# Routed expert rows weighted on ScalarE and summed into the tokens' rows in memory by an accumulating indirect DMA, in place of a gather and weighted sum in the next stage

## The reference, cut to what matters

```python
def _L0_ffn_ref(x, router_w, router_b, routed_w1, routed_w3, routed_w2, shared_w1, shared_w3, shared_w2):
    def _expert(xf, w1, w3, w2):
        return jax.nn.silu(xf @ w1) * (xf @ w3) @ w2
    xf = x.reshape(T, D)
    logits = xf @ router_w + router_b
    topk_vals, topk_idx = jax.lax.top_k(logits, 2)
    sparse = jnp.full_like(logits, -jnp.inf)
    sparse = sparse.at[jnp.arange(T)[:, None], topk_idx].set(topk_vals)
    gates = jax.nn.softmax(sparse, axis=-1)
    routed = jax.vmap(_expert, in_axes=(None, 0, 0, 0))(xf, routed_w1, routed_w3, routed_w2)   # 8 experts
    routed_out = jnp.einsum('etd,te->td', routed, gates)
    shared_out = jax.vmap(_expert, in_axes=(None, 0, 0, 0))(xf, shared_w1, shared_w3, shared_w2).sum(axis=0)   # 2
    return (routed_out + shared_out).reshape(B, S, D)

x = x + tanh(g_xattn[0]) * _L0_xattn_ref(_layernorm(x), ctx, ctx, ...)
x = x + tanh(g_ffn[0]) * _L0_ffn_ref(_layernorm(x), ...)
x = x + tanh(g_xattn[1]) * _L1_xattn_ref(_layernorm(x), ctx)      # softmax(x ctx^T) ctx
x = x + tanh(g_ffn[1]) * _L1_ffn_ref(_layernorm(x), ...)          # quantised up, conv over the sequence, silu, quantised down
```

## Time and profile before

| what | value |
|---|---|
| three runs | 1677.87, 1670.09, 1670.02 us; median 1670.09 |
| profiled execution | 1673.33 us (its span on the core 1671.7) |
| busy over the span | PE 1510.4 us (90%), weight loads 1147.7, DVE 1053.8 (63%), ACT 815.9 (49%), POOL 743.7 (44%) |
| loop over routed tiles | 69 tiles; first output copy at 744.11, last at about 1079 us |

### The profile page before, as it was taken

One profiled execution on the slowest core, in us unless ns is written; L12 is line 12 of the kernel. 1 busy time (PEld: TensorE's weight loads), 2 busy tenths in 40 slices (PEclk: granted clock), 3 DMA queues, 4 the chain that ended last, 5 costly groups with the idle time before them and its releaser, 6 DMA issues. The chain is left out here.

```text
span 1671.7 us, 24835 instructions
## 1 busy us (share of the span) xinstructions
PE 1510.4 (90%) x8764; PEld 1147.7 (69%) x8764; DVE 1053.8 (63%) x1759; ACT 815.9 (49%) x1448; POOL 743.7 (44%) x666
## 2 busy tenths in 40 slices
PE   6589999999978999989999999988888789999997
PEld 5478788788756888867787788765554455555553
DVE  3468878788728564332332333247996899999995
ACT  2145555555522221213343444325777778888883
POOL 0044344435414675243414100255551878888870
PEclk9789999999978999999999999995766889999998
DMA  3157656666326999735535333459772111111112
GB/s 142 46 182 252 210 207 252 228 212 230 127 85 216 355 356 345 247 120 176 179 105 169 119 107 107 138 145 319 235 258 92 38 39 38 64 63 63 52 51 101
DMA packets 131428, 270.31 MB, mean 162 GB/s; under 512 B 16083, under 2 KB 31443, under 8 KB 129288
## 3 DMA queue, kind: packets, MB, share of 16 engines
q1 hardware_dynamic: 100168, 175.47, 31.2%
q0 software_dynamic: 16624, 62.93, 10.7%
q10 hardware_dynamic: 14544, 30.68, 4.9%
HBM read 145.56 MB, written 122.42 MB: 160 GB/s over the span
## 5 line engine op out<-in xcount | busy, mean ns | idle before, releaser
L243 PE MATMUL e_u_ps<-e_xs,w_shared 128*128 128x512 f32 x720 | 169.4, 396 | 6.4 <-DVE e_sg L1262 6.4
L243 PEld LDWEIGHTS e_u_ps<-e_xs,w_shared 128*128 128x128 f32 x720 | 137.6, 192 | 35.4 <-DVE e_sg L1262 6.5
L2357 PE MATMUL f_banks<-b_xdT,w1h 128*128 128x512 f32 x512 | 146.0, 427 | 14.5 <-POOL b_xdT L2107 9.7
L2133 POOL TENSOR_TENSOR b_h<-b_h,b_srow 128x512 f32<-128x512 f32 x112 | 143.3, 1333 | 26.3 <-ACT b_srow L2169 26.3
L1458 PE MATMUL e_u_ps<-e_w,e_xs 128*128 128x512 f32 x528 | 133.0, 401 | 2.0 <-DVE e_xs L1354 1.2
L2357 PEld LDWEIGHTS f_banks<-b_xdT,w1h 128*128 128x128 f32 x512 | 97.1, 196 | 48.2 <-POOL b_xdT L2107 14.1
L2326 PE MATMUL b_o_ps<-w2q,b_h 128*128 128x512 bf16 x448 | 116.9, 384 | 8.7 <-ACT b_h L2163 8.7
L2158 ACT ACTIVATE b_h<-b_h 128x512 f32<-128x512 f32 x128 | 88.2, 690 | 53.4 <-DVE b_h L2248 52.4
L1362 DVE TENSOR_TENSOR e_hT<-e_r_ps,e_hT 128x256 fp32r<-128x256 f32 x69 | 29.3, 424 | 134.5 <-ACT e_hT L1200 134.5
L1458 PEld LDWEIGHTS e_u_ps<-e_w,e_xs 128*128 128x128 f32 x528 | 95.7, 188 | 23.2 <-DVE e_xs L1354 1.6
L2245 DVE SCALAR_TENSOR_TENSOR b_h<-f_banks,cw,b_h 128x511 f32<-128x511 f32 x128 | 95.2, 744 | 22.1 <-ACT b_h L2152 22.1
(11 more groups left out here) (267 smaller groups left out, 3504.5 us busy)
## 6 DMA issues: line engine op xcount, KB each, us to landing
slots_in_scratch<-e_xs SPq DMA_DIRECT2D x22, 1024.0 KB, 8.3
e_xe<-slots_in_scratch SPq DMA_DIRECT2D x69, 256.0 KB, 2.7
experts_out_scratch<-e_ye ACTq DMA_DIRECT2D x69, 256.0 KB, 2.0
yx_a<-in_w POOLq DMA_DIRECT2D x10, 1024.0 KB, 5.9
xin<-in_x SPq DMA_DIRECT2D x16, 512.0 KB, 5.0
xres<-in_x SPq DMA_DIRECT2D x16, 512.0 KB, 5.3
x_scratch<-x SPq DMA_DIRECT2D x32, 256.0 KB, 3.4
xn_scratch<-xn SPq DMA_DIRECT2D x32, 256.0 KB, 2.0
```

What stands on the lines that cost most here:

```text
L243: mm = pe.matmul(n.u_ps[:, (2 * q + j) % 4], ws[q // n.KH][:, pa, at:at + P], xs[:, pb, k], start=(k == 0 and (pa, pb) == PASSES[0]), stop ...
L2133: pool.tensor_tensor(ht, ht, srow[:], ALU.mult).then_inc(u_done, 1)
L2357: mm = pe.matmul(f_ps[:, v % RING], n.w1h[:, k, (c - NV) * P:(c - NV + 1) * P], xdT[:, part, k], start=(k == 0 and part == 0), stop=(k == ...
```

## The change

- A scattered row gets 8 more floats (`meta`, 2080 instead of 2048 bytes): token number, its first slot, two gates, two slots. Unused slots hold zeros and a dummy token number, one of 128 rows added to `x2_d`.
- Before `rx_low(r)`, DVE runs `columns_of(r)`: four instructions on 128x1, which pick the tile's gate (`g_all`) and token numbers (`tok`) out of `xe`. SP's load of the next `xe` waits for them too (`gate_done`).
- ACT's `y_copy` scales by the gate and writes into a ring of four `ye`; it waits for `ye_free`. It issues no store. POOL's `accumulate(r, k)` adds the tile to the token rows of `x2_d` by an indirect DMA with an addition, each waiting for the one before (`summed`). `x2_d` of block 7 is filled with a copy of `x1_d` ahead of the loop, and the last shared block adds to the loaded sums.
- The seven later weight splits leave POOL: in halves of 1536 columns, after the first and the second tile of an expert (`high_half` on ACT, `low_half` on DVE; both halves after the first tile for the last expert). The two splits of experts 3 and 4 in the numbering with shared experts first stay on POOL ahead of `accumulate(0)`. ACT issues the five later pairs of weight loads.
- `ys_d` with its zeroing, gathers, gate copies and combinations go. The fusing stage loads whole rows from `x2_d` into a ring of three buffers and starts with the statistics. ACT and DVE now run it as straight code. The memory for slots is zeroed in pieces of 8 tiles, with small DMAs for the 8 columns.

```diff
-    xs_d = nc.dram_tensor("slots_in_scratch", [MAXT * P, D], F32)
-    ys_d = nc.dram_tensor("experts_out_scratch", [MAXT * P, D], F32)
-    x2_d = nc.dram_tensor("x2_scratch", [T, D], F32)
+    xs_d = nc.dram_tensor("slots_in_scratch", [MAXT * P, D + 8], F32)
+    x2_d = nc.dram_tensor("x2_scratch", [T + P, D], F32)
...
                 sp.wait_ge(rx_full, r)
+                sp.wait_ge(gate_done, r)
...
+            sp.wait_ge(summed, end * 16)
+            for q in fq_out:
+                sp.wait_ge(q, 2 * NC // QB * 16)
+            for b in range(2):
+                sp.dma_start(n.x1[b], n.tile_rows(n.x2_d, b * TB, TB)).then_inc(n.x1_in[b], 16)
+            for t in range(LAST * TB, NT):
+                load_sum(t)
...
+            def accumulate(r, k):
+
+                pool.wait_ge(tok_done, r + 1)
+                pool.tensor_copy(rows[:, k:k + 1], tok[:, ds(r, 1)]).then_inc(rows_done, 1)
+                hold(pool, rows_done, r + 1, n.passed_pool)
+                if not (isinstance(r, int) and r == 0):
+                    hold(pool, summed, r * 16, n.passed_pool)
+                pool.sem_inc(ye_free, 1)
+                hold(pool, y_copied, r + 1, n.passed_pool)
+                pool.indirect_dma_start(out=n.x2_d[:, :], out_offset=bass.IndirectOffsetOnAxis(ap=rows[:, k:k + 1], axis=0),
+                                        in_=ye[:, k], in_offset=None, compute_op=ALU.add).then_inc(summed, 16)
...
+            for e in range(NSH + 1, WB + NSH):
+                pool.wait_ge(y_full, LAST * TB)
                 split(e)
...
+            pool.wait_ge(residual_in, 16)
+            for t in range(LAST * TB - XB, LAST * TB):
+                pool.wait_ge(x2_out[t % XB], t // XB * 16 + 16)
+            quads = (bound(pool, E) + 3) >> 2
+            pool.sem_inc(ye_free, TB)
+            for k in range(TB):
+                accumulate(k, k)
+            with pool.Fori(1, quads) as g:
+                for k in range(TB):
+                    accumulate(g * TB + k, k)
+            hold(pool, summed, quads * (TB * 16), n.passed_pool)
...
+            def high_half(q, half):
+
+                e = q - 1 + WB + NSH
+                cols = slice(half * WN // 2, (half + 1) * WN // 2)
+                if half == 0:
+                    if e - NSH < WB + 2:
+                        act.wait_ge(w_in[e % 2], (e - NSH) // 2 * 32 + 32)
+                    else:
+                        act.wait_ge(w_late[e % 2], (e - NSH - WB) // 2 * 32)
+                act.activation(w[e % WB][:, 0, cols], wraw[e % 2][:, cols], ACT.Copy).then_inc(w_part, 1)
+
+            def fetch(e):
+                for dst, src in n.weights(e % NE, wraw[e % 2]):
+                    act.dma_start(dst, src).then_inc(w_late[e % 2], 16)
+
             def y_copy(r):
                 act.wait_ge(ry_full, r + 1)
-                if not (isinstance(r, int) and r == 0):
-                    act.wait_ge(y_out, r * 16)
-                act.activation(ye[:], y_ps[:, 0], ACT.Copy).then_inc(y_copied, 1)
-                act.wait_ge(y_copied, r + 1)
-                act.dma_start(n.tile_rows(n.ys_d, r), ye[:]).then_inc(y_out, 16)
+                act.wait_ge(gate_done, r + 1)
+                act.wait_ge(ye_free, r + 2)
+                act.activation(ye[:, ds(r & 3, 1)].rearrange("p o d -> p (o d)"), y_ps[:, 0], ACT.Copy,
+                               scale=g_all[:, ds(r, 1)]).then_inc(y_copied, 1)
...
-            end = bound(act, E)
-            with act.Fori(1, end - 1) as r:
-                routed(r, True, False)
+            for q in range(E):
+                final = q == E - 1
+                first_tile, end = bound(act, q) if q else 0, bound(act, q + 1)
+                if q:
+                    routed(first_tile, True, False)
+                    high_half(q, 0)
+                    if final:
+                        high_half(q, 1)
+                    else:
+                        routed(first_tile + 1, True, False)
+                        high_half(q, 1)
+                with act.Fori(first_tile + (1 if final or not q else 2), end - 1 if final else end) as r:
+                    routed(r, True, False)
+                if q and q + WB - 1 + NSH < NE:
+                    act.wait_ge(w_ready, q + WB)
+                    fetch(q + WB + 1 + NSH)
             routed(end - 1, True, True)
...
+            def low_half(q, half):
+                e = q - 1 + WB + NSH
+                cols = slice(half * WN // 2, (half + 1) * WN // 2)
+                dve.wait_ge(w_part, 2 * (q - 1) + half + 1)
+                low = dve.tensor_tensor(w[e % WB][:, 1, cols], wraw[e % 2][:, cols], w[e % WB][:, 0, cols].bitcast(F32),
+                                        ALU.subtract)
+                if half:
+                    low.then_inc(w_ready, 1)
+
+            def columns_of(r):
+
+                dve.wait_ge(xe_in, r * 16 + 16)
+                own = slotid[:, ds(r, 1)]
+                dve.scalar_tensor_tensor(out=g_part[:, 0:1], in0=xe[:, D + 1:D + 2], scalar=own, in1=xe[:, D + 2:D + 3],
+                                         op0=ALU.is_equal, op1=ALU.mult)
+                dve.scalar_tensor_tensor(out=g_part[:, 1:2], in0=xe[:, D + 1:D + 2], scalar=own, in1=xe[:, D + 3:D + 4],
+                                         op0=ALU.not_equal, op1=ALU.mult).then_inc(parts_done, 1)
+                dve.tensor_copy(tok[:, ds(r, 1)], xe[:, D:D + 1]).then_inc(tok_done, 1)
+                dve.wait_ge(parts_done, r + 1)
+                dve.tensor_tensor(g_all[:, ds(r, 1)], g_part[:, 0:1], g_part[:, 1:2], ALU.add).then_inc(gate_done, 1)
+
             def rx_low(r):
+                columns_of(r)
...
-            end = bound(dve, E)
-            with dve.Fori(1, end - 1) as r:
-                routed(r, False)
+            dve.wait_ge(w_ready, WB)
+            for q in range(E):
+                final = q == E - 1
+                first_tile, end = bound(dve, q) if q else 0, bound(dve, q + 1)
+                if q:
+                    routed(first_tile, False)
+                    low_half(q, 0)
+                    if final:
+                        low_half(q, 1)
+                    else:
+                        routed(first_tile + 1, False)
+                        low_half(q, 1)
+                with dve.Fori(first_tile + (1 if final or not q else 2), end - 1 if final else end) as r:
+                    routed(r, False)
             routed(end - 1, True)
...
-                    dve.tensor_copy(gcol[:, o], gate[:, :, ds((s + 1) * TB, TB)]).then_inc(gcol_done, 1)
-                    dve.wait_ge(gcol_done, s + 2)
-                    dve.wait_ge(y_in[o], half_of(s) * 32 * TB + (32 * TB if o else 0))
-                    dve.wait_ge(x2_in[o], half_of(s) * 16 + 16)
-                    combine_first(o)
+                    dve.wait_ge(x1_in[(s + 1) % 3], (s + 1) // 3 * 16 + 16)
+                    stats(0, x1[(s + 1) % 3], mv1_done, s * 2 * TB + TB if mid else 0)
...
-                    combine_second(s, o)
```

More of the change, by code:

```diff
@@ L1225, in _ @@
                 h_high(b, Q - 1)
-            for q in fq_out:
-                act.wait_ge(q, 2 * NC // QB * 16)
+            for q in scattered:
+                act.wait_ge(q, NT // GB * 32)
             rx_high(0)
@@ L1644, in flat @@
                 run(s, s >= 1, 0 <= s < B, s < B - 1, s % 2)
-        def loads(s):
-            return not isinstance(s, int) or 0 <= s < B - 2
         def half_of(s):
```

203 lines of the change are left out of this document (86 added, 117 removed).

## The result

The changed kernel takes 1755.67 us (median of 4 runs, 1752.9 to 1757.5) against 1670.59: a ratio of 1.0493, 95% interval 1.0471 to 1.0514. That is 85 us slower, where 32 were forecast. The profiled execution took 1757.23 us (span 1755.6, 83.9 longer than before). `up` is the first matrix product of a routed tile, and its start marks a period of the loop.

| stretch | before | after | difference |
|---|---|---|---|
| start to the first routed `up` | 732.2 | 741.3 | +9.1 |
| first to last routed `up` (68 periods) | 342.5 | 406.2 | +63.7 |
| last routed `up` to the first output of the fusing stage | 65.7 | 83.5 | +17.9 |
| that output to the last block's (7 periods) | 136.4 | 129.1 | -7.3 |
| from there to the end | 394.9 | 395.5 | +0.6 |

A forecast was written before the change was run, and what follows sets the result against it. TensorE was taken to bound the routed loop, with `rx_low` just in time, and the fusing stage not DVE-bound. Terms 6 + 20 + 8 + 5 + 2 - 4 - 5 = +32 gave 1702 us; 8-in-10 range 1668 to 1750.

The forecast's parts named there:

- POOL's waits are costed at nothing: Routed loop: 72 serial accumulates on POOL add 0 us, hidden by a tile period of about 5.4 us.
- rival B: Routed loop: accumulates bound it, a cycle of 3.4 to 6.1 us against 5.4; 1716 to 1800 us, chance 0.22.
- The sign for "right": Trace signs of the main forecast: among them plain tiles near 5.0 us and accumulates landing in under 5 us.
- B's signs: Routed loop: periods above 5.5 us, with ACT's copy waiting for POOL or a DMA.
- no overlap can rescue it: Accumulates: each must wait for the earlier one's semaphore, so overlapping them cannot shorten the chain; no size of its own.
- End of the loop: Loop's end: 1 MB loads come after the accumulates and no longer delay a tile's store; -4 us, bounds -5 and 0.
- The sum without the chain: Whole kernel: terms sum to +32 us with POOL's waits at nothing, 1702 us as a median.
- the halves: Routed loop: weight splits on ACT and DVE cost 1.4 us for each of 12, with the last expert +20 together.
- the small instructions: Before `rx_low` on DVE: four instructions cost 0.15 us for each of 55 tiles, +8 us, bounds 0 and 17.
- the first three tiles: Loop's start: `y_copy(0)` waits for `ye_free` behind POOL's splits, delaying `down(1)`; 6 us once, bounds 4 and 9.
- Fusing stage: Seven fusing blocks: combinations, gathers and gate copies go, but DVE isn't the bound; 0.67 us a block, -5.
- Rival C: Fusing stage: DVE does bound it, seven blocks each shorten by 5.9 us, -41 for -5; 1666 us, chance 0.15.

The follow-up runs named there:

- the overwriting chain: Changed kernel with the indirect DMA's addition left out, each tile overwriting its tokens' rows, still serial with the same waits: 1702.9 us (one run).
- two in flight: Changed kernel with two accumulates outstanding, an expert's first tile waiting for all before, and no padding tiles: 1701.3 us, ratio 1.017 to the kernel before.
- three kernels: Changed kernel with tiles written to scratch rows by plain DMA (1702.3 us), with the addition left out (1702.9), or with two accumulates outstanding (1701.3).
- the load: Eight idle 128x512 sums on DVE per fusing block, added to the changed kernel with two accumulates outstanding: 1734.2 us, ratio 1.034 to the kernel before.

## Why the prediction was wrong

- **The step that failed** is "POOL's waits are costed at nothing, hidden by a tile period of about 5.4 us", with its test in rival B, "from a landing of 5.1 us on it decides". The landing, 4.8, is inside the bounds taken from the scatters, and by that test it would not have decided. The hand-over was sized at 0.30 from one gap of POOL's queue, which was no wait for a DMA; it is 0.94, and the overwriting chain shows 0.96 where it binds. The cover was right as a mean: with two in flight the tiles behind the first three periods take 5.40 us on average, and 5.14 in most. A link of 5.7 is longer than either, so the chain became the bound. The sign for "right", accumulates that land in under 5 us, came true together with B's signs.
- **B's number is in part luck.** Its formula with the measured link (6.12) gives 1752; measured 1755.7. But by its parts the loop would be some 90 us longer (41 of forecast terms and 50 of chain) and the end 4 shorter; measured +63.7 and +17.9, with 9.1 ahead of the loop. The link of 6.8 us behind its 1799 has no row: its own bounds end at 6.1. And "no overlap can rescue it" is wrong: tiles of one expert never share a row, and two in flight were enough.
- The Trainium skill's size for such a DMA ("DMA: Bandwidth & Descriptors", Anatomy of one DMA), an estimate of 3.2 us in the prediction, fell short of the 4.8 here. For the overwriting scatter's 256 KB the same figures make an estimate of 2.6, and it landed in 2.7. The measurement decides.
- **End of the loop**, forecast -4, was +17.9. "The last accumulate finds room" overlooked that a bound chain arrives with its whole ring behind, and that DVE's wait for it stands ahead of a quarter of the shared block. It goes with the chain: with two in flight this stretch took 61.1 us (65.7 before), which is the forecast's -4.
- **The sum without the chain**, 1702, was met by three kernels (1701 to 1703), but by errors that cancel. Read from one profile each, and taken as adding up, with two in flight: of the 38.2 us by which the loop is longer (380.7 for 342.5) the halves are 12.9 (20 forecast), the small instructions 12.8 (8) and the first three tiles 10.7 (6), by DVE's wait and POOL's subtraction as much as by `ye_free`; 1.8 is left for loads and boundaries (5 and 2). The stretch ahead is 0.4 to 9 (0), the fusing stage -11 (-5).
- **Fusing stage** -7.3 for -5, and -6 to -12 over the profiles of changed kernels without the load. "DVE-bound ... it isn't" was too strong: the last block of the earlier trace rows prepares no successor and is no fair copy of the others. Rival C in full (-41) is excluded.
- **The small instructions**: the 60 ns each of the Trainium skill ("Perfetto Trace Analysis", Optimizing Scalar/DVE Operations) would have cost nothing; 0.24 to 0.27 us a tile says the trace's own durations were the better guide.

## What to carry to other kernels

Price a chain of dependent DMAs as landing plus hand-over, measured from issue to issue, against the period of the tiles that are bound by nothing else. Here two links in flight, where the rows can't meet, were enough. When work leaves a full engine's shadow, look for what stands behind each new wait in program order, and compare the operands' addresses between the two kernels, not only the instructions.

## What was not expected of the hardware

- TensorE's matmuls of 128x128 by 128x512 in fp32 followed every 227 ns with h and x at 192 modulo 512 bytes and every 232 to 234 ns at 288 or 320, at a clock of 1.00. Which modulus counts, and whether it is the address itself or its distance from the other operand's, wasn't tried.
- An addition in an indirect DMA of 128 rows of 2 KB cost 2.1 us of landing and 0.6 us of POOL. From a landing to the next issue it is 0.94 to 0.96 us, with the addition or without; what fills it was not tried.
- DVE's 128x1 instructions with two SBUF operands took up to 4.4 us beside one POOL subtraction, and ended with it (0.21 us otherwise).
